# Packed expert numbers in the first expert loop, and a recurrence with its gate sum split and its products spread

## The reference, cut to what matters

```python
# first expert layer: 16 experts, two groups of four chosen, two experts in each
for e in range(E):
    h = jax.nn.silu(xf @ W1[e]) * (xf @ W3[e])
    out = out + tw[:, e:e + 1] * (h @ W2[e])
...
# recurrence, hidden size 256, five gates; layer 2 takes layer 1's output
def step(carry, gx_t):
    h, c, m = carry
    g = gx_t + h @ Wh
    i, f, c_tilde = sigmoid(g[0]), sigmoid(g[1]), tanh(g[2])
    o, m_new = sigmoid(g[3]), tanh(g[4])
    c_new = f * c + i * c_tilde
    h_new = o * jnp.tanh(c_new) + m_new
```

## Time and profile before

| | |
|---|---|
| time, median of 3 runs | 1110.24 us (1110.03 to 1111.13) |
| time of the profiled execution | 1110.15 us |
| its span in the trace | 1108.2 us |
| expert loop, first product of tile 0 to last `up` product of tile 77 | 237.0 to 489.2 us |
| recurrence, first to last L1508 | 541.9 to 985.2 us |
| granted TensorE clock, mean | 0.923 of full speed |

### The profile page before, as it was taken

The page is one execution under the profiler, slowest core; times in us unless marked ns, Lnnn a source line. Parts: engine busy times, 40 slices in busy tenths (PEclk is TensorE's granted clock), DMA queues, the critical chain, the costliest instruction groups (busy, mean ns, idle before and its releaser), DMA issues.

```text
span 1108.2 us, 43614 instructions
## 1 busy us (share of the span) xinstructions
PE 896.5 (81%) x17230; PEld 721.4 (65%) x17230; DVE 784.1 (71%) x2835; ACT 556.8 (50%) x1629; POOL 331.9 (30%) x481
## 2 busy tenths in 40 slices
PE   3667768267787788773599999999999999989997
PEld 1346545135555555551489999999999988847786
DVE  3458984986655555556678888887788888755877
ACT  0446667125455444532354455555544455545886
POOL 0326656555565565540001111111111111020321
PEclk9769997569999998995699999999999999998999
DMA  8700005201222221216000000000000000002232
GB/s 237 271 1 2 1 30 171 62 25 38 65 66 63 65 65 44 59 34 160 19 4 0 0 0 0 0 0 0 0 0 0 0 0 0 1 2 87 94 140 75
DMA packets 26707, 52.07 MB, mean 47 GB/s; under 512 B 4528, under 2 KB 17816, under 8 KB 26648
## 3 DMA queue, kind: packets, MB, share of 16 engines
q1 hardware_dynamic: 21656, 41.04, 11.3%
q0 software_dynamic: 4992, 10.23, 3.5%
HBM read 44.02 MB, written 7.24 MB: 46 GB/s over the span
## 4 chain that ended last, share of the span: by engine, by line
PE 38%; DVE 10%; issue 7%; ACT 0%; DMA 0%; POOL 0%; DVEq 0%; ACTq 0%
PE quad L1330 19%; PE bank L1330 8%; DVE post L1480 3%; DVE post L1518 2%; PE quad L318 1%; PE bank L318 1%; PE quad L320 1%; PE quad L319 1%; DVE post L1524 1%; PE bank L319 1%; PE bank L320 1%; DVE post L1519 1%; PE quad L1340 1%; PE quad L1628 1%; PE bank L1360 0%
## 5 line engine op out<-in xcount | busy, mean ns | idle before, releaser
L1330 PE MATMUL quad<-post,area 128*128 128x32 f16 (+1 forms) x7520 | 230.2, 182 | 24.7 <-DVE post L1524 18.1
L1330 PEld LDWEIGHTS quad<-post,area 128*128 128x128 f16 x7520 | 213.1, 96 | 41.6 <-DVE post L1524 41.3
L1330 PE MATMUL bank<-post,area 128*128 128x32 f16 (+1 forms) x6260 | 193.2, 180 | 6.7 <-DVE post L1524 4.4
L1330 PEld LDWEIGHTS bank<-post,area 128*128 128x128 f16 x6260 | 176.9, 96 | 12.3 <-DVE post L1524 5.0
L1417 ACT ACTIVATE post<-post 128x96 f32<-128x96 f32 x252 | 71.3, 283 | 171.1 <-DVE post L1480 171.1
L1313 POOL COPY post<-post 128x32 f32 (+1 forms) x126 | 30.8, 245 | 381.8 <-DVE post L1524 381.8
L868 POOL DMA_INDIRECT y_scratch<-area x78 | 76.9, 985 | 88.7 <-DVE area L1209 78.6
L1508 DVE SCALAR_TENSOR_TENSOR post<-post 128x32 f32<-128x32 f32 x252 | 48.4, 192 | 75.6 <-ACT post L1427 75.6
L957 PE MATMUL quad<-w0s,area 128*128 x312 | 61.6, 277 | 49.2 <-DVE area L1209 49.2
L1480 DVE TENSOR_REDUCE post<-bank 128x96 f32<-128x192 f32 x252 | 80.7, 320 | 6.4 <-PE bank L1330 4.8
L1220 DVE SCALAR_TENSOR_TENSOR area<-bank,area 128x512 f32<-128x512 f32 x78 | 53.9, 691 | 43.8 <-ACT area L1033 21.3
(11 more groups left out here) (255 smaller groups left out, 1940.4 us busy)
## 6 DMA issues: line engine op xcount, KB each, us to landing
w0s<-in_w SPq DMA_DIRECT2D x12, 768.0 KB, 12.3
area<-mask_scratch SPq DMA_DIRECT2D x7, 1008.0 KB, 4.6
area<-in_rec SPq DMA_DIRECT2D x7, 640.0 KB
post<-y_scratch SPq DMA_DIRECT2D x16, 252.0 KB
area<-in_w SPq DMA_DIRECT2D x4, 768.0 KB
post<-in_f SPq DMA_DIRECT2D x8, 256.0 KB, 4.4
area<-in_patches SPq DMA_DIRECT2D x1, 1488.4 KB
area<-in_taps SPq DMA_DIRECT2D x1, 1350.0 KB
```

Source lines behind the costliest of these rows:

```text
L1330: mm = pe.matmul(at[0][:, at[1] + out.start:at[1] + out.stop], rec_w[:, w, s, m * P:(m + 1) * P], operand, start=False, stop=False, skip_g ...
```

## The change

Three edits. (1) The experts are packed six to a word: VectorE no longer multiplies `expert_f` by the address step, ScalarE scales the 78 numbers by powers of 16, VectorE sums six at a time into 13 words, and TensorE loads 13 registers once, in the middle of the 64 table products. In the loop the address is computed in registers by a shift, a mask and a multiplication. (2) The sum of y is split in two: o first, m after the new cell; ScalarE makes m last. (3) The products that don't depend on the last step are spread: 12, 12, 18 and 18 to the four places of two passes, where it was 10, 20, 10, 20.

```diff
+WORD = 6
...
             for c in range(COMBOS):
+                if c == COMBOS // 2:
+                    pe.wait_ge(sg("route_dve"), AFTER["expert_at"])
+                    words = [nc.values_load(expert_at[0:1, w:w + 1], engines=(mybir.EngineType.PE,), min_val=0,
+                                            max_val=E0 ** WORD - 1,
...
             def expert_of(i):
-                return nc.values_load(expert_at[0:1, i:i + 1], engines=(mybir.EngineType.PE,), min_val=0,
-                                      max_val=(E0 - 1) * 2 * W0,
...
+                return pe.snap((words[i // WORD] >> 4 * (i % WORD) & E0 - 1) * (2 * W0), min_val=0,
+                               max_val=(E0 - 1) * 2 * W0)
...
+            act.wait_ge(sg("route_pe"), AFTER["expert_ps"])
+            for k in range(WORD):
+                ins = act.activation(expert_row.rearrange("p (w k) -> p k w", k=WORD)[:, k],
+                                     EXPERT[0:1, 0:NT].rearrange("p (w k) -> p k w", k=WORD)[:, k], ACT.Copy,
+                                     scale=float(E0 ** k))
+            ins.then_inc(sg("route_exp"), 1)
...
+                if c == COMBOS // 4:
+                    dve.wait_ge(sg("route_exp"), 2)
+                    link(dve, dve.tensor_reduce(expert_sum, expert_row.rearrange("p (w k) -> p w k", k=WORD), AX, ALU.add))
+                    dve.tensor_copy(expert_at, expert_sum).then_inc(sg("route_dve"), 1)
...
-            dve.wait_ge(sg("route_pe"), AFTER["expert_ps"])
-            dve.tensor_copy(expert_at, EXPERT[0:1, 0:NT]).then_inc(sg("route_dve"), 1)
...
-                    chunks(0, 1 - q, WX0, xcur[:, 1 - q], BOTH, range(odd * GCH // 2, (odd + 1) * GCH // 2))
+                    chunks(0, 1 - q, WX0, xcur[:, 1 - q], BOTH, OM if odd else IFC)
+                if odd and here(t, PAIR, SEQ + 1):
+                    from_first(q, 0, OM)
+                    from_first(q, 1, FIRST)
...
+                    if odd == 0:
+                        from_first(q, 0, IFC)
+                    else:
+                        for which, name in ((IFC[1:], "pre_x1"), (OM, "pre_y1")):
+                            mm = from_first(q, 1, which)
...
                         gates_x(l, n)
-                        gates_y(l, n)
+                        gate_out(l, n)
                         cell_of(l, n)
+                        memory(l, n)
...
                 dve.wait_ge(sg(f"part{l}"), n * 3 - 1)
+                dve.wait_ge(sg(f"tanh_c{l}"), 2 * n)
...
                 if first_layer:
-                    sum_part(0, n0, u, "y")
+                    sum_part(0, n0, u, "y", 0, KH)
...
                     products(0, n0)
                     new_cell(0, n0)
+                    sum_part(0, n0, u, "y", KH, KH)
                     new_state(0, n0, u)
```

More of the change, by code:

```diff
@@ L220, in build @@
         expert_f = view(2, SEQ)
-        expert_at = view(NT, 1).bitcast(I32)
+        expert_row = view(NT, 1)
+        expert_sum = view(NT // WORD, 1)
+        expert_at = view(NT // WORD, 1).bitcast(I32)
         PAIR_AT = at[0]
@@ L910, in ffn_pe @@
             pe.transpose(EXPERT[0:1, 0:SEQ], expert_f[:, 1:2], ident[0:SEQ, 0:SEQ]).then_inc(sg("route_pe"), 1)
+            words = ()
             for c in range(COMBOS):
+                if c == COMBOS // 2:
+                    pe.wait_ge(sg("route_dve"), AFTER["expert_at"])
+                    words = [nc.values_load(expert_at[0:1, w:w + 1], engines=(mybir.EngineType.PE,), min_val=0,
+                                            max_val=E0 ** WORD - 1,
+                                            skip_runtime_bounds_check_because="six experts of four bits each")
+                             for w in range(NT // WORD)]
                 pe.wait_ge(sg("off_hot"), c + 1)
@@ L929, in expert_of @@
             def expert_of(i):
-                return nc.values_load(expert_at[0:1, i:i + 1], engines=(mybir.EngineType.PE,), min_val=0,
-                                      max_val=(E0 - 1) * 2 * W0,
-                                      skip_runtime_bounds_check_because="expert_f is the minimum with the last expert")
+                return pe.snap((words[i // WORD] >> 4 * (i % WORD) & E0 - 1) * (2 * W0), min_val=0,
+                               max_val=(E0 - 1) * 2 * W0)
             def up(i, out, wh, wl, name):
@@ L1332, in chunks, with from_first @@
                 return mm
-            IFC, OM = range(XCH), range(XCH, GCH)
+            IFC, OM, FIRST = range(XCH), range(XCH, GCH), range(1)
+            def from_first(q, k, which):
+                return chunks(1, 1 - q, WX1 + k, hpair0[:, 1 - q, k].rearrange("p s g b -> p (s g b)"), BOTH, which)
             BOTH = slice(0, PAIR * 2 * BATCH)
@@ L1358, in connect @@
                     pe.wait_ge(sg("sum_x0"), SEQ - 2 if j < 2 else SEQ)
-                    pe.wait_ge(sg("sum_y0"), SEQ - 2 if j < 2 else SEQ)
+                    pe.wait_ge(sg("sum_y0"), 2 * (SEQ - 2 if j < 2 else SEQ))
                 mm = pe.matmul(bank[FC_BANK[j]][:, 0:BLK], fc_w[:, k, :],
@@ L1392, in both @@
                             pe.wait_ge(sg("state0"), t)
-                    for which, name in ((IFC, "pre_x1"), (OM, "pre_y1")):
-                        mm = chunks(1, 1 - q, WX1 + odd, hpair0[:, 1 - q, odd].rearrange("p s g b -> p (s g b)"),
-                                    BOTH, which)
-                        if isinstance(t, int) and t == PAIR + 1:
-                            mm.then_inc(sg(name), 1)
+                    if odd == 0:
[3 more added lines that the diff above has]
+                            mm = from_first(q, 1, which)
+                            if isinstance(t, int) and t == PAIR + 1:
+                                mm.then_inc(sg(name), 1)
                 for j, k in FC_AFTER.get(t, ()) if isinstance(t, int) else ():
@@ L1472, in rec_dve, with sum_part @@
             dve.wait_ge(sg("cell_zero"), 2)
-            def sum_part(l, n, u, name):
+            def sum_part(l, n, u, name, first=0, count=XCH):
                 x, y = pair_banks(l, u // PAIR)
-                src, lo, count = (x, 0, XCH) if name == "x" else (y, XCH, GCH - XCH)
+                src, lo = (x, first) if name == "x" else (y, XCH + first)
                 dve.wait_ge(sg(f"pre_{name}{l}"), n)
                 dve.tensor_reduce(pre[:, l, lo * BATCH:(lo + count) * BATCH].rearrange("p (m b) -> p m b", b=BATCH),
-                                  src[:, 0:count * 64].rearrange("p (m s g b) -> p s m b g", m=count, s=PAIR, g=2
-                                                                 )[:, u % PAIR], AX, ALU.add
+                                  src[:, first * 64:(first + count) * 64].rearrange(
+                                      "p (m s g b) -> p s m b g", m=count, s=PAIR, g=2)[:, u % PAIR], AX, ALU.add
                                   ).then_inc(sg(f"sum_{name}{l}"), 1)
```

17 lines of the change are left out of this document (10 added, 7 removed).

## The result

The kernel before takes 1110.4 us, the changed one 1100.1 us (median of 4 executions each): ratio 0.9903, 95% interval 0.9875 to 0.9931. Forecast were 1052 us with a range of 1041 to 1097, so the time lies outside it, 48 us above the forecast. The direction was right, most of the gain didn't come. The profiled execution took 1103.7 us, the longest of its four, with a span of 1101.9 us (before 1108.2).

What follows compares the result with a forecast made beforehand. The prediction took TensorE's late signals to bound the expert loop and a gapless cycle of dependent instructions the recurrence. From 1110.15 us, -44.3 + 4.0 - 18.3 gave 1051.6, so 1052 us, range 1041 to 1097.

Steps and rivals of the forecast that it cites:

- The loads leave the loop: Expert loop: removing TensorE's one load a tile ends its late signals, 207.3 us instead of 251.6, -44.3 us.
- The first rival: Expert loop: gathers or register addresses, not loads, make the signals late, so they stay; 1096 us, chance 0.26.
- the three terms: Expert loop without loads -44.3 us, thirteen loads in the table products +4.0 us, recurrence -18.3 us.
- The next limit: Expert loop without late signals: GpSimd's 2.57 us a tile bounds it, plus 9.4 us for VectorE's weight work.
- The register operations: Two ahead of each expert-loop tile: cost between 0 and 0.302 us, taken as 0.
- Thirteen loads: In the middle of the table products: they delay the first gather, +4.0 us, bounds 0 and 5.7 us.
- The split: Recurrence, sum of y: TensorE's `own` starts 0.075 us earlier in each of 244 half-steps, -18.3 us.
- The spreading: Recurrence: TensorE's fullest half-step falls from 60 to 58 products; gives nothing itself, lets the split give.
- The extra wait for two semaphores: Recurrence, finishing the state: a second wait, if an unhidden VectorE instruction, takes at least 0.10 us.
- the slower rival: Recurrence: an unhidden second wait makes it +0.025 us a half-step, +6 us; 1120 us with late signals, chance 0.03.

Runs made afterwards that it cites:

- number 6: Kernel before with expert-loop phases: fixed experts, gathers or scatters missing, transfers halved or doubled, or TensorE slowed; read tile by tile, the halved-or-doubled kernel once timed at 1108.9 us.
- numbers 1, 3 and 7: Against kernel before: recurrence edits alone 0.9855, packing alone 1.0086; then kernel before rerun unedited 1070.2 us, changed kernel rerun 0.9941; then recurrence edits alone again 0.9870.
- the set of 3: The changed kernel run once more without any edit, against the kernel before on the same chip: 1062.55 us beside 1069.9, ratio 0.9941.

## Why the prediction was wrong

**The step that failed is "The loads leave the loop"**, -44.3 us forecast, -1.7 measured. Its reason for the cause was that "remote" and the load occur in this loop only. What the runs showed in its place: the signals are late without loads and without register addresses (number 6), and with loads they are not late in three of seven sets (numbers 1, 3 and 7). The observation that spoke against the step stood in it, the last tiles with loads and without stalls, and was explained away by needing both. It was the right clue, if only half: there the gathers are missing, and a single transfer a tile, of either kind, makes nothing late; a gather and a scatter do, and two gathers do. Why the signals come late at all stays open. The first rival, the signals stay late, gave 1096 us and was what happened; measured were 1100.1. The 4 us between come of no term: in the trace the three terms are -1.7 + 4.4 - 16.7 = -14.0 us and the rival's -14.3, and what is left is the later start and the slower operations ahead of the loop, which the second trace of the changed kernel doesn't show. The rival's chance of 0.26 was too low for a cause that rested on one trace.

**The next limit** that the prediction saw behind the late signals was wrong too, and hidden by luck. It has 207.3 us for a loop without them, and the changed kernel took 207.2 in the set of 3. But the tile isn't GpSimd's 2.57 us, it is TensorE's 2.50: at 0.07 us a tile GpSimd falls behind little, and its gathers run five tiles ahead. That is 77 x 2.50 = 192.5 us and leaves 14.7 for the tiles with work on weights, where the prediction had 9.4.

**The register operations** were taken as 0, from the last tiles where the sequencer is ahead. That holds in a steady tile (2.50 us with either), not behind a stall: 11 x 0.2 = 2.2 us more where nothing is late. Bounded at 0.302 us a tile the cost was inside its range, the row chosen for it was the wrong one.

**Thirteen loads**: +4.0 forecast, +4.4 and +4.0 measured. Right, and behind the products the first gather doesn't wait for them (4.02 us). The Trainium skill's floor of about 600 ns for a load ("DMA: Bandwidth & Descriptors", Latency and other measured facts) isn't what this chip does here: 0.302 us in the rows, and 4.72 / 13 = 0.36 us from one to the next, the "something between two loads" that the prediction allowed for. The earlier trace rows name VectorE's L1146 as what the 32nd product waited for last, not GpSimd as the prediction has it; the sum doesn't hang on it.

**The split**: -18.3 forecast, -16.7 in the trace, -16.0 and -15.6 in time. The mechanism was right, the link fell by 0.07 us instead of 0.075, the low end of what its two rows allowed.

**The spreading**: 0 by itself, and necessary: both halves right. TensorE's fullest half-step keeps about 4 us of the split's gain without it.

**The extra wait for two semaphores** costs nothing that shows; the slower rival didn't come about.

The sum by the measured terms on a chip without late signals is +4.0 + 2.2 - 16.5 = -10.3 us; -7.4 us was measured, with an interval of -9.2 to -3.5. So 1 us or more is not named. In the two traces of that set it stands behind the recurrence, where no edit reaches: from the last new state to the end 125.9 us in the changed kernel and 123.8 in the one before. In all traces that stretch takes between 122.7 and 127.0 us, and in two of the same kernel (the recurrence edits alone) 125.8 and 122.7, so it need not be a cost of the packing. For the packing alone 6.2 us are named and 8.4 measured, and 6.2 lies in its interval of 6.0 to 12.4.

## What to carry to other kernels

That two things occur only in the same loop is a correlation of one trace; a cause worth 4% of the time deserves a discount until the kernel has been seen without it, and the stretch of the same loop in which the symptom is missing says most. Run the kernel before on more than one chip before explaining a stall that no dependence explains. Work taken off a sequencer counts where the sequencer is behind: read its price right behind a stall, not in the steady state.

## What was not expected of the hardware

The same kernel takes 1070 us in three sets and 1110 to 1117 in four, each execution within 0.6% of its set's median. Every later set had another chip, and no chip was asked twice, so the chip and its state at the time can't be told apart. The difference is in one loop (248.6 against 205.0 us), in signals of TensorE that reach the other engines up to 2.4 us after the recorded end of its work. It is TensorE's signals alone. In 245 to 440 us of the first trace 123 of 260 updates of its semaphores come over 0.3 us after the nearest recorded end, and none of ScalarE's or VectorE's comes more than 0.02 us after it. In the second trace of the same kernel none of TensorE's does either. The ends of products are modelled, so whether the product or only its signal is late isn't shown.

In that state two tiles take 6.4 to 6.5 us, and 0.2 or 0.4 us more of TensorE's work a tile doesn't lengthen them by more than 0.3. Gathers alone at one a tile, scatters alone, or both at half the rate cost no time in it; one burst of four did.

Start times in code that no edit touches moved by up to 5.7 us (205.0 to 210.7 us) from trace to trace, in part with the granted clock ahead of them.
